# Block maxima and exponentials over two score banks per instruction instead of one

## What is computed

```
x = x + tanh(g_xattn) * xattn(layernorm(x), ctx, ctx)
  qp = rope(q @ wq.T); kp = rope(k @ wk.T); vp = v @ wv.T      # split in 16 heads
  scores = qh . kh * sqrt(16), valid where |key - query| <= 64
  attn = softmax(scores over keys); out = (attn @ vh) @ wo.T + b
x = x + tanh(g_ffn) * moe(layernorm(x))     # 16 experts, top 2 per token, 16 slots each
```

## Time and profile before

| | us |
|---|---|
| Median of 3 runs | 1889.34 (1888.83 to 1892.42) |
| The profiled execution | 1888.86 |
| Its span | 1887.1 |
| Attention stage | from the start to about 1259 |
| Score maxima, L496, 512 instructions | 321.1 busy |
| Exponentials, L352, 512 instructions | 264.3 busy |
| Values, L705, 4096 matmuls | 206.1 busy |

### The profile page before, as it was taken

One profiled execution on the slowest core, in us unless ns is written; L12 is line 12 of the kernel. 1 busy time (PEld: TensorE's weight loads), 2 busy tenths in 40 slices (PEclk: granted clock), 3 DMA queues, 4 the chain that ended last, 5 costly groups with the idle time before them and its releaser, 6 DMA issues. The chain is left out here.

```text
span 1887.1 us, 51499 instructions
## 1 busy us (share of the span) xinstructions
PE 1528.9 (81%) x16844; PEld 1200.2 (64%) x16844; DVE 1483.6 (79%) x3249; ACT 1165.1 (62%) x2321; POOL 1023.6 (54%) x1234
## 2 busy tenths in 40 slices
PE   4888888888888888888888888961597888788870
PEld 3566666666666666666666666640487777777760
DVE  3788888888888888888888888859788888888863
ACT  3777677777777776777777777742364555555530
POOL 3545555545545454555555545427346677677755
PEclk9999999999999999999999999975699999999995
DMA  2121212122121212121212122420257777777775
GB/s 87 46 84 56 83 56 76 63 71 68 65 74 57 82 56 83 56 83 56 83 56 81 58 68 71 137 89 12 62 170 224 231 240 236 229 240 236 239 212 178
DMA packets 156085, 210.12 MB, mean 111 GB/s; under 512 B 18688, under 2 KB 104832, under 8 KB 156032
## 3 DMA queue, kind: packets, MB, share of 16 engines
q1 hardware_dynamic: 143744, 175.92, 28.8%
q0 software_dynamic: 12288, 33.57, 6.4%
HBM read 125.54 MB, written 83.89 MB: 111 GB/s over the span
## 5 line engine op out<-in xcount | busy, mean ns | idle before, releaser
L496 DVE TRANSPOSE_TENSOR_REDUCE part_max<-ST 128x16 f32<-128x512 f32 x512 | 321.1, 684 | 151.0 <-PE ST L678 151.0
L705 PE MATMUL PO<-probs_t,v_aug 128*32 128x128 f32 x4096 | 206.1, 285 | 79.1 <-ACT probs_t L352 59.2
L352 ACT ACTIVATE probs_t<-ST 128x512 f32<-128x512 f32 x512 | 264.3, 602 | 8.6 <-PE ST L693 8.6
L705 PEld LDWEIGHTS PO<-probs_t,v_aug 128*32 128x32 f32 x4096 | 84.9, 108 | 194.8 <-ACT probs_t L352 188.2
L312 POOL TENSOR_TENSOR q_rest<-q_rot,q_head 128x512 f32<-128x512 f32 x64 | 82.5, 1289 | 217.3 <-ACT q_head L405 217.3
L295 POOL TENSOR_TENSOR k_rot<-k_cos,k_sin 128x256 f32<-128x256 f32 x64 | 47.2, 737 | 259.0 <-DVE k_sin L534 259.0
L1171 ACT ACTIVATE eo<-EO 128x512 f32<-128x512 f32 x128 | 76.6, 598 | 177.6 <-DMA eo_d<-eo 177.1
L1150 POOL DMA_INDIRECT first<-eo_d,collect_row x128 | 123.3, 963 | 107.1 <-DVE y_sb L1237 84.3
L1253 PE MATMUL GU<-we_hi,s_hi 128*128 128x256 f32 x512 | 156.2, 305 | 0.1
L1150 POOL DMA_INDIRECT second<-eo_d,collect_row x128 | 125.4, 980 | 42.8 <-issue 36.3
L1254 PE MATMUL GU<-we_hi,s_lo 128*128 128x256 f32 x512 | 145.5, 284 | 0.0
(11 more groups left out here) (158 smaller groups left out, 5731.0 us busy)
## 6 DMA issues: line engine op xcount, KB each, us to landing
eo_d<-eo SPq DMA_DIRECT2D x128, 256.0 KB, 2.6
x_in_sb<-x SPq DMA_DIRECT2D x64, 256.0 KB, 2.8
c_in_sb<-ctx_t SPq DMA_DIRECT2D x64, 256.0 KB, 2.8
xr_sb<-x SPq DMA_DIRECT2D x64, 256.0 KB, 4.0
x_d<-x SPq DMA_DIRECT2D x64, 256.0 KB, 4.0
xn_d<-xn SPq DMA_DIRECT2D x64, 256.0 KB, 4.2
scaled<-xn_d SPq DMA_DIRECT2D x128, 128.0 KB
scaled<-x_d SPq DMA_DIRECT2D x128, 128.0 KB
```

The costliest lines, as they stand in the source:

```text
L352: act.activation(probs_t[:, b, i].rearrange("p j q -> p (j q)"), ST[i][:], ACT.Exp) \
L496: dve.tensor_reduce(part_max[:, i, 0], ST[i][:].rearrange("p (c l) -> p c l", l=32), AX_X, ALU.max, apply_transpose=True).then_inc(M["part ...
L705: last = pe.matmul(PO[32 * j:32 * j + 32, i * SEQ:(i + 1) * SEQ], v_aug[:, n.par, b, head], probs_t[:, b, i, j], start=True, stop=True)
```

## The change

The four score banks become two PSUM tensors of two banks each, at the same places. `partial_max` takes two banks with each instruction, after the mask of the second one is done; `exp_units` takes two banks with each instruction, after the subtraction from the second one is done, and gives both counts of `probs_done` at its end. TensorE's instructions and its waits stay as they are: unit 0 still waits for the first count of `probs_done` and unit 1 for the second, which now come together.

```diff
--- before.py
+++ after.py
@@ -163,7 +163,8 @@
     gates = T["gates"]
     logits = T["logits"]
 
-    ST = [pb(f"ST{i}") for i in range(4)]
+    wide = [ctx.enter_context(nc.psum_tensor(f"ST{i}", [P, 2, 512], F32)) for i in range(2)]
+    ST = [wide[i // 2][:, i % 2] for i in range(4)]
     PO = pb("PO")
     F0, F1, F2 = pb("F0"), pb("F1"), pb("F2")
 
@@ -345,12 +346,12 @@
         act.activation(w_hi[:].rearrange("p a k e -> p (a k e)"), stage.rearrange("p a k e -> p (a k e)"), ACT.Copy) \
             .then_inc(M["w_split"], 1)
 
-        def exp_unit(n, b, i):
-
-            act.wait_ge(M["shifted"], seq(n, b) * 4 + i + 1)
-            wait_for(act, M["pv_done"], (seq(n, b) - 2) * 4 + i + 1)
-            act.activation(probs_t[:, b, i].rearrange("p j q -> p (j q)"), ST[i][:], ACT.Exp) \
-                .then_inc(M["probs_done"], 1)
+        def exp_units(n, b, h):
+
+            act.wait_ge(M["shifted"], seq(n, b) * 4 + 2 * h + 2)
+            wait_for(act, M["pv_done"], (seq(n, b) - 2) * 4 + 2 * h + 2)
+            act.activation(probs_t[:, b, 2 * h:2 * h + 2].rearrange("p i j q -> p (i j q)"),
+                           wide[h][:].rearrange("p i c -> p (i c)"), ACT.Exp).then_inc(M["probs_done"], 2)
 
         def copy_out_t(n, b):
             act.wait_ge(M["pv_done"], seq(n, b) * 4 + 4)
@@ -446,8 +447,8 @@
             if (s - 1).real:
                 attention_head(s - 1)
             if s.real:
-                for i in range(4):
-                    exp_unit(s, 0, i)
+                for h in range(2):
+                    exp_units(s, 0, h)
                 copy_out_t(s, 0)
             if (s - 2).real:
                 copy_normed2_t(s - 2)
@@ -463,8 +464,8 @@
             if (s + 1).real:
                 query_rests(s + 1)
             if s.real:
-                for i in range(4):
-                    exp_unit(s, 1, i)
+                for h in range(2):
+                    exp_units(s, 1, h)
             if (s + 2).real:
                 input_head(s + 2)
             if s.beyond == 0:
@@ -491,10 +492,10 @@
         def partial_max(n, b):
 
             wait_for(dve, M["turned_done"], seq(n, b))
-            for i in range(4):
-                dve.wait_ge(M["scores_done"], seq(n, b) * 4 + i + 1)
-                dve.tensor_reduce(part_max[:, i, 0], ST[i][:].rearrange("p (c l) -> p c l", l=32), AX_X, ALU.max,
-                                  apply_transpose=True).then_inc(M["part_done"], 1)
+            for h in range(2):
+                dve.wait_ge(M["scores_done"], seq(n, b) * 4 + 2 * h + 2)
+                dve.tensor_reduce(part_max[:, 2 * h:2 * h + 2, 0], wide[h][:].rearrange("p i (c l) -> p i c l", l=32), AX_X,
+                                  ALU.max, apply_transpose=True).then_inc(M["part_done"], 2)
 
         def shift_of(n, b):
 
@@ -690,7 +691,7 @@
             pe.wait_ge(M["shift_done"], seq(n, b) + 1)
             for i in range(4):
                 rows = slice(32 * i, 32 * i + 32)
-                pe.matmul(ST[i][:], ones[rows], shift[rows].rearrange("p c l -> p (c l)"), start=False, stop=True,
+                pe.matmul(ST[i], ones[rows], shift[rows].rearrange("p c l -> p (c l)"), start=False, stop=True,
                           skip_group_check=True).then_inc(M["shifted"], 1)
 
         def values_unit(n, b, i):
```

## The result

The changed kernel took 1968.67 us in the median (1962.61 to 1971.46), against 1889.93 for the kernel before: a ratio of 1.041, 95% interval 1.039 to 1.044. It is slower, as forecast, but by 79 us and not by 14; the time lies far outside the range. The profiled execution took 1971.46 us, its span is 1969.7. Nearly all of the loss is in the attention stage: VectorE's last instruction of `normalise` starts at 1259.6 us before and at 1339.3 after, 79.7 us later, and the whole span is 82.6 us longer.

The account below looks back on a forecast made before the run. TensorE's order was taken as the bound, with one stretch per half through ScalarE's exponentials. 64 x 0.16 + 35 x 0.10 + 29 x 0 gave +13.7 us on 1888.86, so 1902.6; range 1891 to 1914.

Parts of the forecast that it names:

- The bound: Attention stage: TensorE's order sets the period, passing through ScalarE's exponentials once in each half; saved engine time has slack.
- The sizes of the wide instructions: ScalarE and VectorE: a wide exponential 1.03 us, two 1.94 against 2.06; two wide maxima 2.37 against 2.51.
- The order of the value units: TensorE's value units run in twos behind each release: next scores +0.16 us in half 0, +0.10 in half 1 without a turn.
- the middle of the bounds: Half 1 at the loop's turn, 29 times: scores between 0.12 us sooner and 0.10 later, taken as nothing.
- The wait for both subtractions: Before the wide exponentials: the four subtractions run together in 0.50 us while ScalarE is busy, so nothing is added.
- The clock: Steady attention stage: TensorE's granted clock noted as full; the sum has no term for a change of it.
- Absorbed (1): TensorE's idle 0.42 and 0.26 us before L717 and L693 in half 1 absorb half 0's 0.16: 1892.4 us, chance 0.13.
- Faster (2): If the period ran through the last exponential on ScalarE, each half gains 0.12 us: -15.4, 1873.5 us, chance 0.11.
- VectorE (3): A wide maximum costs 1.37 us, half 0's maxima end 0.33 later: +0.22 us a pair, 1916.7 us, chance 0.06.
- the bank edge (4): A wide exponential is no cheaper across banks, 1.09 us and 2.06 for both: +25.0 us, 1913.9, chance 0.06.
- The 0.32 us to spare of the maxima in half 0: Half 0: maxima end at 1014.43, TensorE reaches their transposition at 1014.75 after its projections, so wide maxima cost nothing.

Follow-up runs that it names:

- the filled kernel: The whole change plus overwritten 512-column matmuls where TensorE waits for the first wide exponential, five in half 0 and three in half 1: 1906.36 us, ratio 1.008.
- half 1 only: The whole change plus three additional matmuls in TensorE's wait of half 1, none in half 0: 1911.60 us, ratio 1.009.
- one matmul in half 1: The whole change plus one additional matmul, about 0.21 us, in TensorE's wait of half 1: 1915.03 us, ratio 1.014.
- Four kernels: The change (1968.67 us); wide exponentials alone (1971.03); all narrow, TensorE waiting for exponentials in twos (1969.94); the change with five matmuls in half 0's wait (1961.87).

## Why the prediction was wrong

**The bound, right.** TensorE's order sets the step, and the wide instructions' saving of engine time is not felt. The wide maxima alone measured 1.000.

**The sizes of the wide instructions, right.** 1.03 us forecast and 1.02 found for an exponential, 1.94 and 1.94 for two; 2.37 and 2.38 for two maxima.

**The order of the value units, right.** +0.16 in half 0 and +0.10 in half 1 without a turn: the trace of after has 2.81 against 2.82 in half 0, the filled kernel 2.57 against 2.57 in half 1. At a turn the middle of the bounds was taken, nothing; measured is -0.08, near the lower bound of -0.12.

**The wait for both subtractions, mis-sized.** "Nothing is added", since the four run together and ScalarE is in L418 or L393 until then. The wide exponential starts 0.08 to 0.09 us later in each half, 64 x 2 x 0.09 = 11.5 us; 0.034 of it is the second count, the rest a later start behind it. The cover was read off overlapping rows: L393 ends at 1016.81 and the exponentials start at 1016.76, so the end of a ScalarE row isn't what the next one waits for; and a modelled matmul end of 0.50 was taken for the release. The distance of 0.62 in both halves would have told. With it and the turn the sum is 13.7 + 11.5 - 29 x 0.08 = 22.9 us, 1911.8. The change with its clock kept is at 1906.36 (both waits filled), 1911.60 (half 1 only) and 1915.03 (one matmul in half 1), +15, +18 and +27 against their bases. Their steps are 0.35 to 0.38 us longer in the mean, 22 to 24 us for 64 full ones, and in their traces the attention stage ends 20.0, 23.4 and 26.2 us later than before (1279.6, 1282.9 and 1285.8 against 1259.6).

**The clock, the step that failed.** The prediction noted "a full granted clock" and carried it into the sum as a constant. It moved TensorE's wait in half 1 from 0.18 to 0.69 us, just behind gaps of 0.42 and 0.26, and asked only what is late afterwards, not what TensorE does when it has been idle longer. Against their own bases the change loses 79 us and the three kernels with the clock kept lose 15, 18 and 27: the clock is worth 52 to 64 us, two thirds to four fifths of the loss. None of the rivals had it. The Trainium skill, "TensorE: Matmul & The Clock Gate", section "Part 1: The HAM clock gate (the "warmup" mystery)", says that the clock is set by how busy the engine has been recently, at half when it idled, and that activity releases it; the trace agrees in the two levels and in the return, 0.50 from 1011.72 to 1015.11 behind the gap and 1.00 later. It should have been the rival that ends far out: rows 1 show 2.1 us idle of each 19.1, and a full clock at that point says nothing on how much more it stands.

**The rivals.** Absorbed (1): no, the gaps before L718 and L694 stay at 0.42 and 0.26. Faster (2): no, the scores follow the last release by the two units' time. VectorE (3) and the bank edge (4): no, by the sizes above. The 0.32 us to spare of the maxima in half 0 was read too simply, since VectorE has `normalise` between them and the next step of the chain; the measured 2.38 us is short enough to make no difference.

**What stays open.** Why the clock falls only when the wait ends in the last 0.28 us ahead of a moment of the grid. Nor do the runs tell how the several gaps of half 1 share in it, since only the last one was filled, and no run has it between 0.18 and 0.66 us without a matmul in it. Why a wide exponential starts 0.05 us later behind its count than a narrow one is open too.

## What to carry to other kernels

Before two instructions that feed another engine are made one, look at when that engine gets its first input and how much work then stands behind the last release: 0.12 us sooner at the end was worth less than 0.43 us later at the start. Where TensorE waits in a kernel at full clock, a longer wait can be priced twice, as a wait and as a risk to the clock of what follows, here 0.85 to 1.13 us for each fall; in this kernel one matmul in a gap of 0.7 us removed the second price, and work from elsewhere in the step may do the same. Wider instructions on an engine that isn't the bound gained nothing: the maxima, which delayed no input, changed VectorE's busy time and nothing else.

## What the runs showed of the hardware

- The granted clock fell to half behind a TensorE gap of 0.66 to 0.70 us that followed gaps of 0.42 and 0.26, and was 0.50 for 3.39 us although TensorE was then fully busy. In the steady stages it never fell with the last gap at 0.18 us or with 0.2 us of it filled. A gap of 1.28 to 1.29 us, elsewhere in the same step, did no harm.
- The changes of the granted clock lie on an even grid in each trace. All 210 falls of the steady stages came 0.02 to 0.28 us after the gap's end; in the 159 steps where the next moment of the grid was 0.30 us or more away, none came.
- Four kernels settle at the same step of 20.48 us (single steps 20.43 to 20.53), where each fall brings the next; 0.43 us more work in each step brought the loss of one of them from 79 us down to 62, and 0.25 us less work to 17, which also counts 16 us for the work itself.
- The counts of four matmuls that run together on different row groups came 0.034 us apart, with the rows showing one common length of 0.50 us. A narrow exponential started 0.11 to 0.12 us after the count that released it, one of two banks 0.165 to 0.175.
- A turn of the hardware loop cost TensorE's stream 0.45 us behind four units released one by one, and 0.27 behind units released in twos; counted from the last release to the next scores it is 0.81 and 0.85 us in all, which would fit a turn that runs in part while the last units do. In steps with a fall it is not seen (20.44 to 20.52 in every step).
